# A two-block network on one core: LSTM steps that carry the second half of the layers before them

## The reference

```python
def step(carry, xs):
    h, c = carry
    xi_t, xf_t, xg_t, xo_t = xs
    i_t = sigmoid(xi_t + h @ V_i)
    g_t = tanh(xg_t + h @ V_c)
    o_t = sigmoid(xo_t + h @ V_o)
    c_new = h * c + i_t * g_t
    h_new = o_t * tanh(c_new)
    return (h_new, c_new), h_new
```

## Time and profile before

| | us |
|---|---|
| median of 3 timed runs | 577.79 (577.62 to 578.49) |
| the profiled execution | 573.73 |
| its span, first to last instruction | 571.9 |
| PE busy | 525.1 (92%) |
| DVE busy | 287.0 (50%) |
| ACT busy | 219.2 (38%) |
| POOL busy | 104.2 (18%) |
| mean granted PE clock | 0.985 |
| 201.4 of the PE time | fills in the LSTM (L678, 720 matmuls) |

### The profile page before, as it was taken

One profiled execution on the slowest core, in us unless ns is written; L12 is line 12 of the kernel. 1 busy time (PEld: TensorE's weight loads), 2 busy tenths in 40 slices (PEclk: granted clock), 3 DMA queues, 4 the chain that ended last, 5 costly groups with the idle time before them and its releaser, 6 DMA issues.

```text
span 571.9 us, 10803 instructions
## 1 busy us (share of the span) xinstructions
PE 525.1 (92%) x3813; PEld 300.3 (53%) x3813; DVE 287.0 (50%) x1329; ACT 219.2 (38%) x1086; POOL 104.2 (18%) x103
## 2 busy tenths in 40 slices
PE   7799999999999999997999999999999999999996
PEld 3588888888574233674544444444444444444443
DVE  4966666666556537206344444444444444444443
ACT  2456555555327450101233333333333333333332
POOL 7387777777110000000000000000000000000000
PEclk9999999999989999999699999999999999999998
DMA  7500000000000000000000000000000000000000
GB/s 216 218 2 0 2 1 2 2 1 1 1 1 1 2 0 0 1 0 1 1 1 2 2 1 2 1 1 2 2 1 1 2 2 1 1 2 1 2 1 19
DMA packets 2872, 7.12 MB, mean 12 GB/s; under 512 B 1405, under 2 KB 1986, under 8 KB 2626
## 3 DMA queue, kind: packets, MB, share of 16 engines
q1 hardware_dynamic: 2818, 6.44, 3.3%
HBM read 6.18 MB, written 0.26 MB: 11 GB/s over the span
## 4 chain that ended last, share of the span: by engine, by line
PE 51%; DVE 24%; ACT 16%; issue 7%; DMA 0%; DVEq 0%; ACTq 0%
PE bk L662 14%; DVE bk L1169 9%; ACT gi L833 8%; DVE mem L1172 7%; ACT bk L837 7%; PE bk L547 5%; PE bk L619 4%; PE bk L565 2%; PE bk L477 2%; PE bk L458 2%; PE bk L436 2%; PE bk L446 2%; PE bk L361 2%; PE bk L354 1%; PE bk L309 1%
## 5 line engine op out<-in xcount | busy, mean ns | idle before, releaser
L678 PE MATMUL bk<-idle 128*64 128x512 bf16 x720 | 201.4, 386 | 0.0
L662 PEld LDWEIGHTS bk<-mem,lvh 65*64 65x64 f32 x1536 | 81.2, 138 | 145.6 <-DVE mem L1172 144.0
L662 PE MATMUL bk<-mem,lvh 65*64 65x4 f32 x1536 | 104.0, 207 | 23.4 <-DVE mem L1172 4.3
L833 ACT ACTIVATE gi<-bk 128x4 f32<-128x4 f32 x256 | 44.9, 175 | 151.8 <-PE bk L662 151.8
L1169 DVE TENSOR_TENSOR_SCAN bk<-gi 64x12 f32<-64x12 f32 x256 | 47.5, 186 | 107.4 <-ACT gi L833 107.4
L678 PEld LDWEIGHTS bk<-idle 128*64 128x64 bf16 x720 | 61.3, 112 | 22.9 <-issue 1.2
L1172 DVE SCALAR_TENSOR_TENSOR mem<-og,bk 64x4 f32<-64x4 f32 x256 | 38.4, 150 | 53.7 <-ACT bk L837 53.7
L837 ACT ACTIVATE bk<-bk 64x4 f32<-64x4 f32 x256 | 36.6, 143 | 40.9 <-DVE bk L1169 40.5
L1176 DVE SCALAR_TENSOR_TENSOR gi<-mem,bk 64x4 f32<-64x4 f32 x255 | 39.1, 153 | 8.8
L835 ACT ACTIVATE og<-bk 64x4 f32<-64x4 f32 x256 | 42.8, 167 | 0.1
L922 DVE TENSOR_TENSOR mem<-mem,bk 128x256 f32<-128x256 f32 x64 | 27.0, 422 | 17.2 <-PE bk L354 11.4
(11 more groups left out here) (270 smaller groups left out, 695.0 us busy)
## 6 DMA issues: line engine op xcount, KB each, us to landing
cw<-in_cw SPq DMA_DIRECT2D x1, 3456.0 KB, 10.9
w<-in_w SPq DMA_DIRECT2D x1, 520.0 KB
mem<-in_memw SPq DMA_DIRECT2D x1, 512.0 KB, 3.4
w<-in_w SPq DMA_DIRECT2D x1, 512.0 KB
xm<-in_xm SPq DMA_DIRECT2D x1, 256.0 KB, 2.8
xs<-in_x SPq DMA_DIRECT2D x1, 256.0 KB, 3.7
out<-xs SPq DMA_DIRECT2D x1, 256.0 KB, 2.0
consts<-in_consts SPq DMA_DIRECT2D x1, 134.0 KB, 2.7
```

Source lines behind the costliest of these rows:

```text
L662: return nc.tensor.matmul(bk[row:row + D, 2 * (s // CH % 2) + k, c:c + B], lvh[:, g, :], hist[:, s, :], start=False, stop=True, skip_group ...
L678: nc.tensor.matmul(bk[0:D, 5, 0:FILL_N], idle[:, 0:D], idle[:, 128:128 + FILL_N], start=True, stop=True)
L833: nc.scalar.activation(gi[:, 2:2 + 3 * B:3], bk[:, bank, cols], ACT.Tanh).then_inc(sem("in_gate"), 1)
```

## The change

The tokens of the second 512 columns are ordered so that the image rows 8 to 11 come first and 12 to 15 last (`tokens`, `place`). Then:

- Experts g = 8 to 15 work on the 256 tokens of rows 8 to 11 only. The 256 tokens of rows 12 to 15 go through the eight experts in LSTM steps 1 to 27, three steps per expert: up projection and gelu of one half, the same of the other half with the spread, then the copy of the spread weights by ACT, after which POOL multiplies. The down projection follows three steps later. Their sum is added in steps 28 to 30.
- The 1x1 convolution takes 12 of 16 rows, the 3x3 kinds take 11, 11, 9, 10, 9 and 8 rows, and chain and last norm the even tiles (rows 0 to 7). The remaining rows are done in the steps: norm of the odd tiles in steps 31 to 43 on DVE (root by shift and three Newton iterations), the rest of the 1x1 convolution to step 47, two taps per step in steps 48 to 81, chain in steps 83 to 86, norm in steps 87 to 99, transposes and copies to step 102.
- Late work of a step is issued by each engine after the step's own instructions. The fills are left out in every step with late work on PE, and in all steps 1 to 29 and 48 to 81.
- `t3T` is filled in four parts: positions 0 to 63 by DVE before step 0, 64 to 127 by ACT in step 0, the rest by ACT in steps 101 and 102. The cell's tanh goes to bank 4, the fills to bank 7. ACT loads gelu's table instead of tanh's ahead of the LSTM.
- Add-back and statistics of the even tiles stand inside the expert loop (g = 12 to 14).

```diff
+LATE = 1
+BACK = LATE + 3 * E + 4
+NORM2 = BACK + 2
+CONV = NORM2 + 17
+POST = CONV + 35
+NORM3 = POST + 4
...
+        def tokens(g):
+
+            return slice(0, 512) if g < E else slice(512, 768) if g < 2 * E else slice(768, 1024)
+
+        def width(g):
+
+            return 512 if g < E else 256
...
+            for e in range(E):
+                pool.wait_ge(sem("hT"), (2 * E + e + 1) * HC)
+                pool.wait_ge(sem("late_sp"), e + 1)
+                nc.gpsimd.tensor_tensor(hT[:, e, :, 0:256], hT[:, e, :, 0:256], mid(spS[e % 2][:, :], HC), ALU.mult).then_inc(sem("late_hw"), 1)
...
-                    nc.tensor.matmul(bk[:, 4 + k % 4, :], w1g[:, g % E, c * 128:(c + 1) * 128],
-                                     x2A[:, g // E * 512:(g // E + 1) * 512], start=True, stop=True).then_inc(sem("hid_ps"), 1)
+                    nc.tensor.matmul(bk[:, 4 + k % 4, 0:width(g)], w1g[:, g % E, c * 128:(c + 1) * 128],
+                                     x2A[:, tokens(g)], start=True, stop=True).then_inc(sem("hid_ps"), 1)
...
-            taps(0, 0, img[0], True, False)
-            taps(0, 1, img[1], False, True).then_inc(sem("z_ps"), 1)
-            taps(1, 3, img[1], True, False)
+            taps(0, 0, img[0], 0, 11, range(9), True, False)
+            taps(0, 1, img[1], 0, 11, range(9), False, True).then_inc(sem("z_ps"), 1)
+            taps(1, 3, img[1], 0, 9, range(9), True, False)
             pe.wait_ge(sem("z"), 1)
-            taps(0, 2, zim[0], False, True).then_inc(sem("z_ps"), 1)
+            taps(0, 2, zim[0], 0, 10, range(9), False, True).then_inc(sem("z_ps"), 1)
             pe.wait_ge(sem("z"), 2)
-            taps(1, 4, zim[0], False, True).then_inc(sem("z_ps"), 1)
+            taps(1, 4, zim[0], 0, 9, range(9), False, True).then_inc(sem("z_ps"), 1)
             pe.wait_ge(sem("z"), 3)
-            taps(1, 5, zim[1], False, True).then_inc(sem("z_ps"), 1)
+            taps(1, 5, zim[1], 0, 8, range(9), False, True).then_inc(sem("z_ps"), 1)
...
+            def late_expert(e, j):
+
+                if j < 2:
+                    if e == 0 and j == 0:
+                        pe.wait_ge(sem("t3T_far"), 1)
+                    else:
+                        pe.wait_ge(sem("hT"), (2 * E + e) * HC + j)
+                    nc.tensor.matmul(bk[:, 5, 0:256], w1g[:, e, j * 128:(j + 1) * 128], x2A[:, tokens(2 * E)], start=True,
+                                     stop=True).then_inc(sem("hid_ps"), 1)
+                if j == 1:
+                    if e:
+                        pe.wait_ge(sem("late_sp"), e)
+                    nc.tensor.matmul(bk[:, 6, 0:256], sel[:, e * 128:(e + 1) * 128], W3[:, tokens(2 * E)], start=True,
+                                     stop=True).then_inc(sem("spread"), 1)
+
+            def late_down(e):
+
+                if e == 0:
+                    nc.tensor.matmul(bk[0:D, 7, 0:256], b2[:, :], W8T[:, tokens(2 * E)], start=True, stop=False, skip_group_check=True)
+                pe.wait_ge(sem("late_hw"), e + 1)
+                for c in range(HC):
+                    ins = nc.tensor.matmul(bk[c * D:(c + 1) * D, 7, 0:256], w2[:, e, c, :], hT[:, e, c, 0:256],
+                                           start=(e == 0 and c == 1), stop=(e == E - 1), skip_group_check=True)
+                if e == E - 1:
+                    ins.then_inc(sem("down"), 1)
...
+                i, v = u // 5, u % 5
+                ks = range(2 * v, min(2 * v + 2, 9))
+                if i == 0:
+                    if v == 0:
+                        pe.wait_ge(sem("img"), 4)
+                    taps(6, 0, img[0], 10, 16, ks, True, False)
...
+            def late(s):
+
+                m = s - LATE
+                if 0 <= m < 3 * E and m % 3 < 2:
+                    late_expert(m // 3, m % 3)
+                elif 5 <= m < 3 * E + 3 and m % 3 == 2:
+                    late_down(m // 3 - 1)
+                elif s == BACK:
+                    pe.wait_ge(sem("late_yT"), 1)
...
+                elif CONV <= s < CONV + 20:
+                    late_taps(s - CONV)
+                elif CONV + 21 <= s < CONV + 26:
+                    late_taps(s - CONV - 1)
+                elif CONV + 27 <= s < CONV + 32:
+                    late_taps(s - CONV - 2)
...
+                if late(s) or LATE <= s <= BACK or CONV <= s < CONV + 34:
+                    fills = 0
+                if s % CH == 2 and s // CH == 3:
+                    pe.wait_ge(sem("t3T_far"), 1)
+                if s % CH == 2 and s // CH == 7:
+                    pe.wait_ge(sem("t3T_far"), 3)
...
-            table(ACT.Tanh)
+            table(ACT.Gelu)
...
+            def late(s):
+
+                m = s - LATE
+                if 0 <= m < 3 * E and m % 3 < 2:
+                    e, c = m // 3, m % 3
+                    if m == 0:
+                        act.wait_ge(sem("down"), 2 * E)
+                    act.wait_ge(sem("hid_ps"), (2 * E + e) * HC + c + 1)
+                    nc.scalar.activation(hT[:, e, c, 0:256], bk[:, 5, 0:256], ACT.Gelu,
+                                         bias=b1p[:, e * HC + c:e * HC + c + 1]).then_inc(sem("hT"), 1)
+                elif 0 <= m < 3 * E:
+                    e = m // 3
+                    act.wait_ge(sem("spread"), 2 * E + e + 1)
+                    if e >= 2:
+                        act.wait_ge(sem("late_hw"), e - 1)
+                    nc.scalar.copy(spS[e % 2][:, :], bk[:, 6, 0:256]).then_inc(sem("late_sp"), 1)
...
+                if g == E + 4:
+                    add_back(0)
+                if g == E + 5:
+                    link(stats(range(0, NT, 2)))
+                if g == E + 6:
+                    link(moments(range(0, NT, 2)))
...
+            def late_norm(u, eps):
+
+                if u in (0, 1):
+                    link(stats((4 * u + 1, 4 * u + 3)))
+                elif u in (2, 3):
+                    link(moments((4 * u - 7, 4 * u - 5)))
+                elif u == 4:
+                    link(nc.vector.tensor_scalar(lv4, mv[:, O2, 1], eps, None, ALU.add))
+                    link(nc.vector.tensor_scalar(ls4.bitcast(I32), lv4.bitcast(I32), 1, None, ALU.logical_shift_right))
...
+                elif s == POST:
+                    dve.wait_ge(sem("late_A3"), 2)
+                    link(products(1))
+                elif s == POST + 1:
+                    link(sums(1))
+                    link(heads(1))
+                elif s == POST + 2:
+                    link(chained(1))
+                elif s == POST + 3:
+                    link(add_conv(1))
+                elif NORM3 <= s < NORM3 + 13:
+                    late_norm(s - NORM3, 1e-5)
```

More of the change, by code:

```diff
@@ L15 @@
 F32 = mybir.dt.float32
+I32 = mybir.dt.int32
 ALU = mybir.AluOpType
@@ L182, in build @@
         yT = [sb(f"yT{n}", [128, NTOK // 2]) for n in range(2)]
+        spS = [sb(f"spS{n}", [128, NTOK // 4]) for n in range(2)]
         fold = sb("fold", [128, D])
@@ L804, in _ @@
             act.wait_ge(sem("W8T_ps"), 1)
[L805 to L806 removed]
+            nc.scalar.copy(W8T[:, 0:512], bk[0:E, 0, :]).then_inc(sem("W8T"), 1)
+            nc.scalar.copy(W8T[:, 512:1024].rearrange("p (a j s) -> p a j s", a=2, j=4), halves_of(bk[0:E, 1, :])).then_inc(sem("W8T"), 1)
             for g in range(3, 2 * E):
@@ L1126, in _ @@
             add_back(1)
-            norm(xs[:, :, :], xn[:, :, :], 1e-6, "ln")
-            dve.wait_ge(sem("ln"), 2)
-            nc.vector.tensor_tensor(xs[:, :, :], xs[:, :, :], xn[:, :, :], ALU.add)
-            for k, (need, bank) in enumerate(((1, 0), (2, 0), (3, 1))):
+            link(stats(range(1, NT, 2)))
+            link(moments(range(1, NT, 2)))
+            nc.vector.tensor_scalar(rs[:, :], mv[:, :, 1], 1e-6, None, ALU.add).then_inc(sem("var"), 1)
+            nc.vector.tensor_tensor(xc[:, :, :], xs[:, :, :], wide(mv[:, :, 0], D), ALU.subtract)
@@ new lines, in products, with sums, heads @@
+            def products(c):
+                h = slice(B * c, B * c + B)
+                return nc.vector.tensor_tensor(prod[:, h, 1:D + 1], A3[:, h, :], mid(w3[:, :], B), ALU.mult)
+            def sums(c):
+                h = slice(B * c, B * c + B)
+                return nc.vector.tensor_reduce(st[:, h], prod[:, h, 1:D + 1], AX, ALU.add)
+            def heads(c):
+                h = slice(B * c, B * c + B)
+                return nc.vector.tensor_scalar(prod[:, h, 0:1], wide(st[:, h], 1), -1.0, b3n[:, 0:1], ALU.mult, ALU.add)
@@ new lines, in _ @@
+            link(heads(0))
+            link(chained(0))
+            link(add_conv(0))
+            E2, O2 = slice(0, NT, 2), slice(1, NT, 2)
+            link(stats(range(0, NT, 2)))
+            link(moments(range(0, NT, 2)))
+            nc.vector.tensor_scalar(rs[:, :], mv[:, :, 1], 1e-5, None, ALU.add).then_inc(sem("var"), 1)
+            nc.vector.tensor_tensor(xc[:, E2, :], xs[:, E2, :], wide(mv[:, E2, 0], D), ALU.subtract)
+            rstd()
```

(1 more changed line is left out.)

261 lines of the change are left out of this document (195 added, 66 removed).

## The result

The changed kernel takes 582.42 us (median of 14 runs, 579.92 to 589.97), the kernel before 578.09 (14 runs on the same chip, 576.17 to 582.25). The ratio is 1.0087, with a 95% interval of 1.0059 to 1.0115. It is 0.9% slower, where I had forecast 563.1 and a range of 553 to 574. The profiled execution of after took 589.04 us (span 587.0), that of before 573.73. About 10 us of this distance lie ahead of everything that the change touches: TensorE's clock fell three times there in this execution, once in that of before. 589.04 is one of the two slowest of the 14 runs. So I compare the two traces from the first spread of expert weights on.

What follows compares the result with a forecast made beforehand. It took the LSTM's chain of waits as the bound, 256 steps of 1.14 us. Stages ahead gave -25.5, LSTM terms +10.8: 573.73 profiled became about 559.0, plus 4.06 for the median gave 563.1 us, range 553 to 574.

Steps and rivals of the forecast that it cites:

- Stages ahead of the LSTM: Experts, convolutions, norms, chain and transposes before step 0, halved or cut in columns: 25.5 us less.
- The slow start: First six LSTM steps, 1.57 us each at half clock before: full clock at step 0 gives 2.6 us back.
- The held scan: LSTM scan waits for GpSimd's late multiply once per expert, 0.76 us each for eight experts: 6.1 us more.
- Gelu: Late gelu on ScalarE delays the next gate tanh by 0.05 us, 16 times: 0.8 us more, bounds 0 and 7.5.
- VectorE's pairs: Late VectorE operations before the next scan overrun, pairs by about 0.05 us: 1.5 us over about 30 steps, bounds 0.5 and 4.
- table loads: Gelu and tanh mixed on ScalarE in the steps: priced at nothing; as a rival 41 us of loads, near 604, 2%.
- The clock: LSTM steps without fills: half clock after step 25, recovery 2.6 us, convolution steps 2.4: 5.0 us more, bounds 0 and 27.
- slower than before: Rival, 4%: PE at half clock in all 63 steps without fills, each 1.57 us, 27.1 more: 588.
- The two rivals that end slower: Half clock in all 63 steps without fills (4%, 588), and ScalarE table loads in the steps (2%, near 604).
- half clock from the first expert on: Rival, 19%: late up projections take 0.85 us, two of three expert steps grow to 1.6, 0.75 per expert: 569.

Runs made afterwards that it cites:

- both_safe: Changed kernel with 128-wide fills back in all 63 steps, three ahead of step 0, late multiply on VectorE; 551.84 to 553.36 us, two of six runs 601.5 and 608.5.
- stages_only: Changed kernel without the late work of steps 1 to 102 (output incomplete) and with three fills in every step; 548.26 us, ratio 0.9462.
- pool_safe: As both_safe, but the late multiply left on GpSimd as in the changed kernel; 558.92 and 560.30 us, two other runs 585.95 and 599.63.
- before_nofill: Kernel before with nothing moved, only the fills left out in steps 1 to 29 and 48 to 81; 583.90 us, ratio 1.0086.
- both_two: As both_narrow, with two 512-column fills instead of three in steps without late work; 596.68 us, ratio 1.0287.
- experts_narrow: As both_narrow, with fills kept in steps 1 to 29 but left out in steps 48 to 81; 569.67 us, ratio 0.9862.
- convs_narrow: As both_narrow, with fills left out in steps 1 to 29 but kept in steps 48 to 81; 564.81 us, ratio 0.9801.
- multiply_dve: Changed kernel with the late multiply moved from GpSimd to VectorE in two pieces reading PSUM, no fills added; 580.22 us, ratio 1.0034.
- both_narrow: As both_safe, with fills 64 columns wide instead of 128; 555.87 and 556.31 us, two other runs 582.03 and 583.94.
- experts_only: As both_safe, with fills left out in steps 48 to 81; 591.99 to 594.22 us in three runs, 572.74 in the fourth.
- fills_kept: Changed kernel with 128-wide, 256-column fills beside late work, three more ahead of step 0, late experts' sum altered; 560.27 to 562.79 us, a fourth run 622.91.
- before_wide: Kernel before, order unchanged, with LSTM fills 128 instead of 64 wide and three more ahead of step 0; 576.53 us, one of ten runs 613.46.

## Why the prediction was wrong

- **Stages ahead of the LSTM, -25.5: right.** Measured -26.2 between the two traces, and step 0 of both_safe begins 25.1 earlier than before (248.16 against 273.25 in the earlier trace rows). The convolutions' 108 passes took 15.1 us with their tails (7.74 + 2.61 + 2.47 + 2.27), for 14.1 forecast. In the same count they took 24.2 before, so they gave 9.1 where I had 9.5. (The forecast calls 128 columns, 0.107, "still no shorter than a weight load", 0.114. They are shorter; its sum takes 0.114.)
- **The slow start, -2.6: right.** Step 0 runs at full clock in after, and in stages_only, where nothing follows to bring the clock down, 2.4 come back.
- **The held scan, +6.1: right in kind and near in size, hidden where it was.** Seven scans were held, not eight, by 0.43 to 0.69 each in after, for 0.76 forecast. In after it is worth under 2 us (14.9 against 13.1 us in steps 0 to 29), since PE is late by as much. At full clock six of seven were held by 0.78 (pool_safe).
- **Gelu, VectorE's pairs, table loads.** No table load stands inside the steps. VectorE's late operations of the norms, the router and the chain cost 2.9 us at full clock (both_safe: 1.3 in steps 30 to 47, 1.6 from 82 to 109; I gave 1.5, bounds 0.5 and 4): a pair is 0.06, as forecast, but it stands in 24 steps, and three single ones take 0.35 to 0.4 each. I took 1.5 for about 30 steps, so this term was half of what it should be. Gelu is within its bounds: all of steps 0 to 29 cost 1.9 in both_safe.
- **The clock, +5.0: wrong, and this is the step that failed.** I took 1.00 through the expert steps and a fall in steps 25 to 28, "I give 34 x 0.07 = 2.4" for the convolutions, and 2.6 for the recovery. Measured: 0.50 from step 2 on, and again from step 46. After (582.4) against pool_safe (559.6), which differ in the fills alone, is 22.8 us, where I had 5.0. The rest of my sum holds: without the clock term it gives 558.1, and pool_safe less its two short spells is 556.7.

Two mistakes lie in that term. One is the place: I read the earlier trace rows as if only a quiet stretch brought the lower clock, and took the late work for a substitute of the fills. In this kernel it isn't: PE was busy for 2.46 of the 3 us before the first fall, and the same late work with fills beside it stays at 1.00 in both_safe. (That after has PE busy for 47.45 of 51 us at 0.50 doesn't tell how busy it would be at full clock, since each matmul takes longer there.) The other is the size: I priced a late step by its matmuls at full clock plus a few hundredths. At half clock a convolution step needs 0.51 + 1.10 = 1.61 on PE, 0.47 more than the chain's 1.14, not 0.07. An up projection with its spread needs 2.00.

The rival "slower than before" (4%, 588) names what happened: half clock in all 63 steps, decided from 40 on. It priced this at 27.1 (63 steps at 1.57); the runs show 22.8. Against it I had put that the new steps "carry less" than three fills. They do, in columns, but a step at half clock takes as long with them (1.61 against 1.57). And carrying less spoke for the rival: less work on PE is what goes with the lower clock here, as before_nofill and both_two show. (The two rivals that end slower add up to 6%, not the 0.05 stated.) The rival "half clock from the first expert on" (19%, 569) had the place right for the first half and took a late expert at 0.75; it is 1.6 with its scan free (13.1 us over 8).

Of what brings the lower clock, the runs show this: in before_nofill it fell at 340.5, in the second step without fills, when PE had paused for no more than 0.75 us at a time, and stayed at 0.50 with PE busy for 16.70 of 31.5 us. So no long pause is needed. The Trainium skill (TensorE: Matmul & The Clock Gate, A second HAM failure mode: psum-queue depth-cycling) says of another kernel that small idle times between groups of matmuls are enough to make the clock swing; by that reading the clock term would have been taken for all 63 steps, and the trace agrees that short pauses can do it. But the reading alone does not tell which steps will fall: the kernel before pauses too (PE busy 107.07 of 117 us in the earlier trace rows) and stays at 1.00 there. Where between the two the limit lies, these runs don't tell.

## What to carry over

Fills that keep TensorE's clock up are part of the kernel's work: when real matmuls are moved into their place, keep fills beside them and look at the granted clock before anything else, since PE can be busy for nearly all of a stretch and be at half clock (here 47.45 of 51 us). Price every step that loses its fills at both clock levels, as PE's work in it at half clock against the chain's length. Here the two spells took 13.6 and 8.7 us of the 26 that the shorter stages bring: either alone leaves a gain (experts_narrow, convs_narrow), both together none (multiply_dve, after). Moving the last work off an engine pair that blocks the chain (here GpSimd beside the scan) is worth its full price only once PE no longer covers it.

## What the hardware showed that I had not expected

- In the kernel after, the clock fell within two steps of the LSTM's start (259.1) though the fills ahead had run until 254.9 and PE was busy for 2.46 of the 3 us before.
- Two fills of 512 columns per step did not hold the clock where three did (both_two and both_narrow, from step 30 on).
- A spell can go on long after the fills are back, where they don't fit a half-clock step: 123 us in experts_only (308.7 to 431.6), with PE busy 80.66 of 84 us.
- Most versions with fills in the late steps have runs of two kinds: 552 and 601 to 608 for both_safe, 556 and 582 to 584 for both_narrow, 561 and 623 for fills_kept. So has before_wide (613 in one of ten), which has no late work, so late work isn't needed for it. The kernel before stays within 573.7 to 583.2. For these four no trace of a slower run was kept. How to make the fast version hold in every run is open.
